# Conv and routed attention on one core: each pair of heads in its own half of the array

## The reference

```python
x = conv3x3(quantize(x), sign(W) * mean|W|) + b
xn = layernorm(x, g1, b1)
q, k, v = split(xn @ wqkv + bqkv)            # 64 channels each
qr, kr, vr = to_regions(q, k, v)             # 49 regions (7x7) of 64 pixels (8x8)
idx = top_k(mean(qr) @ mean(kr).T, 4)        # 4 key regions for each query region
scores = einsum(qh, kh[idx]) / sqrt(8)       # 8 heads of 8 channels, 64 queries x 256 keys
x = x + (softmax(scores) @ vh[idx]) @ wo + bo
x = x + gelu(layernorm(x, g2, b2) @ w1 + bm1) @ w2 + bm2
```

## Time and profile before

| what | value |
|---|---|
| median of three runs | 5610.56 us |
| profiled execution, its own time | 5625.85 us |
| its span | 5623.2 us |
| mean granted TensorE clock | 0.898 |
| 98 steps of a pair, from the first score product at 247.4 us on | about 338 us |

### The profile page before, as it was taken

The page is one execution under the profiler, slowest core; times in us unless marked ns, Lnnn a source line. Parts: engine busy times, 40 slices in busy tenths (PEclk is TensorE's granted clock), DMA queues, the critical chain, the costliest instruction groups (busy, mean ns, idle before and its releaser), DMA issues.

```text
span 5623.2 us, 182695 instructions
## 1 busy us (share of the span) xinstructions
PE 4720.9 (84%) x43666; PEld 3049.9 (54%) x43666; DVE 3648.9 (65%) x8855; ACT 3287.3 (58%) x6282; POOL 2777.4 (49%) x9656
## 2 busy tenths in 40 slices
PE   2388888888889898888888889888888888888888
PEld 1265555655556555555555556555565655556564
DVE  2266666766667666676766667666676766667676
ACT  1156556565665756556565665656556565665657
POOL 1245455454554645455454554545455464554553
PEclk9589899988889989898989999989899998999989
DMA  2333343333423334243333423334233333423311
GB/s 61 95 99 92 82 109 75 94 84 91 108 68 102 82 93 103 72 109 83 96 87 89 109 69 101 82 94 104 71 110 88 94 84 92 111 65 106 83 45 33
DMA packets 626961, 494.05 MB, mean 88 GB/s; under 512 B 483792, under 2 KB 613968, under 8 KB 615536
## 3 DMA queue, kind: packets, MB, share of 16 engines
q10 hardware_dynamic: 335360, 212.04, 16.6%
q1 hardware_dynamic: 290416, 268.94, 16.5%
HBM read 268.80 MB, written 211.94 MB: 85 GB/s over the span
## 4 chain that ended last, share of the span: by engine, by line
PE 52%; DMA 13%; issue 9%; ACT 7%; DVE 6%; DVEq 4%; SPq 4%; ACTq 3%; POOL 2%; POOLq 0%
PE ps L1003 11%; PE ps L1033 9%; PE ps L1017 8%; DMA max_d<-tr 6%; PE ps L896 5%; DMA qm<-qk_d 3%; DVEq L223 3%; PE ps L953 3%; ACTq L237 2%; PE ps L989 2%; PE ps L916 2%; PE ps L912 2%; DMA xin<-in_x 2%; ACT pt L847 2%; PE ps L974 2%
## 5 line engine op out<-in xcount | busy, mean ns | idle before, releaser
L736 DVE TENSOR_REDUCE mx<-ps 128x4 f32<-128x1024 f32 x1568 | 1921.6, 1225 | 1396.2 <-PE ps L1003 1128.7
L847 ACT ACTIVATE pt<-ps 128x512 f32<-128x512 f32 x3136 | 1694.2, 592 | 875.0 <-PE ps L1017 811.9
L505 POOL COPY vg<-vs 64x72 f32 x6272 | 1563.5, 249 | 781.6 <-POOL kg L490 576.7
L1003 PE MATMUL ps<-kg,qm 96*128 96x256 f32 x6272 | 1358.3, 342 | 364.4 <-DVE mx L736 112.2
L490 POOL CAST kg<-ks 96x128 fp32r x3136 | 845.2, 295 | 1550.5 <-PE ps L1017 1195.5
L1003 PEld LDWEIGHTS ps<-kg,qm 96*128 96x128 f32 x6272 | 963.3, 206 | 1087.2 <-issue 889.0
L1017 PE MATMUL ps<-qm,kg 97*128 97x256 f32 x6272 | 1126.5, 303 | 151.7 <-ACT pt L847 96.9
L1033 PE MATMUL ps<-pt,vg 128*32 128x128 f32 x25088 | 1092.0, 294 | 51.8 <-DVE um L726 39.1
L1017 PEld LDWEIGHTS ps<-qm,kg 97*128 97x128 f32 x6272 | 940.2, 206 | 214.6 <-ACT pt L847 154.7
L1033 PEld LDWEIGHTS ps<-pt,vg 128*32 128x32 f32 x25088 | 629.5, 114 | 296.5 <-issue 58.0
L645 DVE CAST kg<-ks 96x128 fp32r x3136 | 630.9, 244 | 137.9 <-issue 132.4
(11 more groups left out here) (113 smaller groups left out, 4036.1 us busy)
## 6 DMA issues: line engine op xcount, KB each, us to landing
qk_d<-stg SPq DMA_DIRECT2D x224, 448.0 KB, 3.6
qm<-qk_d ACTq DMA_DIRECT2D x1792, 42.0 KB
ks<-qk_d ACTq DMA_DIRECT2D x96, 784.0 KB, 6.3
vs<-v_d ACTq DMA_DIRECT2D x64, 882.0 KB, 7.1
xin<-in_x SPq DMA_DIRECT2D x119, 224.0 KB, 2.6
xi_d<-xi SPq DMA_DIRECT2D x112, 224.0 KB, 2.7
qk_d<-stg SPq DMA_DIRECT2D x112, 224.0 KB, 3.2
max_d<-tr SPq DMA_DIRECT2D x1568, 2.0 KB
```

The lines of the kernel that those rows point to most:

```text
L505: j = pool.tensor_copy(vg[slot][rows, (k // 2) * VW:(k // 2 + 1) * VW], vs[place(m)[0]][rows, bass.ds(region, 1), :].rearrange("p o n -> p ...
L736: v.tensor_reduce(mx[h % 2][:].rearrange("p (g j e) -> p g j e", g=2, j=2)[:, :, :, 0], ps[:, 0:2, :].rearrange("p g (j k) -> p g j k", j= ...
L847: act.activation(pt[m % 2][:, c], ps[:, 2 + c, :], ACT.Exp, scale=float(HD) ** -0.5).then_inc(S["pt_ready"], 1)
L1003: i = pe.matmul(ps[:, g, 256 * j:256 * j + 256], qm[c % 2][0:NP3, t, g, 2 * j:2 * j + 2, :].rearrange("p h t -> p (h t)"), kg[slot][0:NP3, ...
```

## The change

Heads are taken in pairs. A pair takes 48 rows (`NP3` = 3 * 2 * 8), and the two pairs of a group lie in the two halves of the array: rows 0 to 47 and 64 to 111 (`HALF` = 64). `qm` becomes half as large: in each half it has column blocks for two heads. `ks` has its rows in the same places, and its unused rows are set to -1, so the copies into `kg` now take all 128 rows and bring the -1 rows (48 and 112) with them. `scores` still issues four products, now of 48 rows, where consecutive ones lie in different halves and write different banks. `turned` issues eight products of 49 rows with 128 moving columns in place of four of 97 rows with 256; a bank now belongs to a half of the array, not to two of the key regions, so all eight must be done before either bank is full, and they start only when both banks' exps of the step before are done. The keys come in six DMAs in place of three, issued every step and not every second step. The row of largest scores goes to two rows of 256 numbers.

```diff
--- before.py
+++ after.py
@@ -28,7 +28,8 @@
 EPS = 1e-5
 HG = 4
 NG = HEADS // HG
-NP3 = 3 * HG * HD
+HALF = 64
+NP3 = 3 * 2 * HD
 VC = 18
 VW = 4 * VC
 
@@ -49,7 +50,7 @@
 ROUTE_AT = 62
 A_LOAD, B_LOAD = 70, 6
 QK_DMAS, V_DMAS = 3, 4
-KV_DMAS = 5
+KV_DMAS = 8
 
 
 def p_item(h):
@@ -141,7 +142,7 @@
 
         ks = [sb(f"ks{i}", [128, NG, R, RT], F32R) for i in range(2)]
         vs = [sb(f"vs{i}", [128, R, VW]) for i in range(2)]
-        qm = [sb(f"qm{i}", [128, NW, NG, HG, RT], F32R) for i in range(2)]
+        qm = [sb(f"qm{i}", [128, NW, NG, 2, RT], F32R) for i in range(2)]
         kg = [sb(f"kg{i}", [128, NG, TOPK, RT], F32R) for i in range(RING)]
         vg = [sb(f"vg{i}", [128, 2 * VW + 16]) for i in range(RING)]
         mx = [sb(f"mx{i}", [128, 32]) for i in range(2)]
@@ -234,16 +235,18 @@
             i, s = c // NW, c % NW
             src = qk_d[bass.ds(q, 1), i, 0:C, :, ST * s:ST * s + ST].rearrange("o (g h d) q (s t) -> g h (o d q) s t", g=NG, h=HG, s=NW)
             for g, h in heads:
-                eng.dma_start(qm[c % 2][24 * h:24 * h + 24, :, g, h, :].bitcast(F32), src[g, h]).then_inc(q_loaded[c % 2], 16)
+                row = HALF * (h // 2) + 24 * (h % 2)
+                eng.dma_start(qm[c % 2][row:row + 24, :, g, h % 2, :].bitcast(F32), src[g, h]).then_inc(q_loaded[c % 2], 16)
 
         def keys_values(eng, q, i, n):
 
-            if n < 3:
-                src = qk_d[bass.ds(q, 1), i, C:2 * C, n // 2, :].rearrange("o (g c) n -> (o c) g n", g=NG)
-                dst = ks[i][n:NP3:3].rearrange("p g r t -> p g (r t)").bitcast(F32)
+            if n < 6:
+                part, term = n // 3, n % 3
+                src = qk_d[bass.ds(q, 1), i, C:2 * C, term // 2, :].rearrange("o (g j c) n -> j (o c) g n", g=NG, j=2)[part]
+                dst = ks[i][HALF * part + term:HALF * part + NP3:3].rearrange("p g r t -> p g (r t)").bitcast(F32)
             else:
                 src = v_d[bass.ds(q, 1), i].rearrange("o t r n -> (o t) (r n)")
-                dst = vs[i][64 * (n - 3):64 * (n - 3) + 64].rearrange("p r n -> p (r n)")
+                dst = vs[i][64 * (n - 6):64 * (n - 6) + 64].rearrange("p r n -> p (r n)")
             eng.dma_start(dst, src).then_inc(kv_loaded[i], 16)
 
         def loads(eng, p, h, kind):
@@ -259,14 +262,14 @@
                 if h == A_LOAD:
                     staged_all(eng, p + 1)
                     gathered(eng, p, R)
-                if 0 <= h - A_LOAD < 2 * KV_DMAS and (h - A_LOAD) % 2 == 0:
-                    keys_values(eng, p + 1, 0, (h - A_LOAD) // 2)
+                if 0 <= h - A_LOAD < KV_DMAS:
+                    keys_values(eng, p + 1, 0, h - A_LOAD)
             local = h if kind == "lead" else h - STEPS
             if local >= 0 and kind != "last":
                 if local == B_LOAD and kind != "lead":
                     gathered(eng, p, STEPS)
-                if 0 <= local - B_LOAD < 2 * KV_DMAS and (local - B_LOAD) % 2 == 0:
-                    keys_values(eng, p if kind == "lead" else p + 1, 1, (local - B_LOAD) // 2)
+                if 0 <= local - B_LOAD < KV_DMAS:
+                    keys_values(eng, p if kind == "lead" else p + 1, 1, local - B_LOAD)
 
         def first_loads(eng):
 
@@ -361,8 +364,8 @@
 
                     sp.wait_ge(hopped[m % 2], (p * R + m // 2 + 1) * 16)
                     settled(sp)
-                    sp.dma_start(qm[m // NW % 2][NP3:NP3 + 1, m % NW].rearrange("o g h t -> o (g h t)").bitcast(F32),
-                                 max_d[m % RING].rearrange("j p -> (j p)").unsqueeze(0)).then_inc(row_ready[m % RING], 16)
+                    sp.dma_start(qm[m // NW % 2][NP3:128:HALF, m % NW].rearrange("o g e t -> o (g e t)").bitcast(F32),
+                                 max_d[m % RING].rearrange("(j g) p -> j (g p)", j=2)).then_inc(row_ready[m % RING], 16)
                 if live(h, kind):
 
                     sp.wait_ge(S["tr_ready"], T + 1)
@@ -487,8 +490,8 @@
                     pool.wait_ge(kv_loaded[i], (p + m // STEPS + 1) * (16 * KV_DMAS))
                     settled(pool)
                 for k, region in enumerate(chosen(m, 2)):
-                    j = pool.tensor_copy(kg[slot][0:NP3, :, 2 + k, :],
-                                         ks[place(m)[0]][0:NP3, :, bass.ds(region, 1), :].rearrange("p g o t -> p g (o t)"))
+                    j = pool.tensor_copy(kg[slot][:, :, 2 + k, :],
+                                         ks[place(m)[0]][:, :, bass.ds(region, 1), :].rearrange("p g o t -> p g (o t)"))
                 j.then_inc(S["kp_ready"], 1)
 
             def values(p, m, kind):
@@ -589,8 +592,8 @@
                 v.memset(t[:], 1.0)
             for t in qm:
                 v.memset(t[:].rearrange("p s g h t -> p (s g h t)").bitcast(F32), 0.0)
-            for t in kg:
-                v.memset(t[:].rearrange("p g k t -> p (g k t)").bitcast(F32), -1.0)
+            for t in ks:
+                v.memset(t[:].rearrange("p g r t -> p (g r t)").bitcast(F32), -1.0)
             link(v.memset(rx[:], 0.0))
             v.memset(epst, EPS)
             v.memset(mean_w[0:64, 0:64], 1.0 / C)
@@ -642,8 +645,8 @@
                     settled(v)
                 gather_ready(v, p, m)
                 for k, region in enumerate(regions(v, regs, m, 0, 2)):
-                    j = v.tensor_copy(kg[slot][0:NP3, :, k, :],
-                                      ks[place(m)[0]][0:NP3, :, bass.ds(region, 1), :].rearrange("p g o t -> p g (o t)"))
+                    j = v.tensor_copy(kg[slot][:, :, k, :],
+                                      ks[place(m)[0]][:, :, bass.ds(region, 1), :].rearrange("p g o t -> p g (o t)"))
                 j.then_inc(S["kd_ready"], 1)
 
             def strip_ahead(q, h):
@@ -1000,9 +1003,9 @@
                     pe.wait_ge(S["mx_ready"], T)
                 for g in range(NG):
                     for j in range(2):
-                        i = pe.matmul(ps[:, g, 256 * j:256 * j + 256],
-                                      qm[c % 2][0:NP3, t, g, 2 * j:2 * j + 2, :].rearrange("p h t -> p (h t)"),
-                                      kg[slot][0:NP3, g].rearrange("p k t -> p (k t)"), start=True, stop=True)
+                        d = slice(HALF * j, HALF * j + NP3)
+                        i = pe.matmul(ps[:, j, 256 * g:256 * g + 256], qm[c % 2][d, t, g].rearrange("p e t -> p (e t)"),
+                                      kg[slot][d, g].rearrange("p k t -> p (k t)"), start=True, stop=True)
                 i.then_inc(S["sm_full"], 1)
 
             def turned(p, m):
@@ -1010,14 +1013,17 @@
                 T = p * STEPS + m
                 c, t, slot = m // NW, m % NW, m % RING
                 pe.wait_ge(row_ready[slot], (p * 14 + c + 1) * 16)
+                if not (isinstance(T, int) and T == 0):
+                    pe.wait_ge(S["pt_ready"], (T - 1) * 2 + 2)
                 for b in range(2):
-                    if not (isinstance(T, int) and T == 0):
-                        pe.wait_ge(S["pt_ready"], (T - 1) * 2 + b + 1)
                     for g in range(NG):
-                        i = pe.matmul(ps[:, 2 + b, 256 * g:256 * g + 256],
-                                      kg[slot][0:NP3 + 1, g, 2 * b:2 * b + 2, :].rearrange("p k t -> p (k t)"),
-                                      qm[c % 2][0:NP3 + 1, t, g].rearrange("p h t -> p (h t)"), start=True, stop=True)
-                    i.then_inc(S["st_full"], 1)
+                        for j in range(2):
+                            d = slice(HALF * j, HALF * j + NP3 + 1)
+                            n = 256 * b + 128 * g
+                            i = pe.matmul(ps[:, 2 + j, n:n + 128], kg[slot][d, g, 2 * b:2 * b + 2, :].rearrange("p k t -> p (k t)"),
+                                          qm[c % 2][d, t, g].rearrange("p e t -> p (e t)"), start=True, stop=True)
+                            if b == 1 and g == 1:
+                                i.then_inc(S["st_full"], 1)
 
             def attended(p, m):
 
@@ -1032,7 +1038,7 @@
                     for j in range(4):
                         i = pe.matmul(ps[32 * j:32 * j + 32, 4, 128 * u:128 * u + 128],
                                       vg[slot][:, c * VW + VC * j:c * VW + VC * j + 32],
-                                      pt[m % 2][:, c, 128 * j:128 * j + 128], start=c == 0, stop=c == 1)
+                                      pt[m % 2][:, j % 2, 256 * c + 128 * (j // 2):256 * c + 128 * (j // 2) + 128], start=c == 0, stop=c == 1)
                 i.then_inc(S["u_full"], 1)
 
             def step(p, h, kind):
```

## The result

The changed kernel is slower: 6057.71 us (median of four runs, 6021.98 to 6092.67) against 5611.55 us in the same comparison, a ratio of 1.079 with a 95% interval of 1.0721 to 1.0859. The forecast was 5490 us, range 5340 to 5690. The profiled execution took 6092.67 us with a span of 6090.9, and its mean granted TensorE clock is 0.780, where it was 0.898.

What follows compares the result with a forecast made beforehand. Bound: TensorE's written order in full steps, a 2.2 us loop in short ones, SyncE's queue close behind. Terms -222 - 55 + 33 + 75 + 30 + 10 + 5 = -124 us from 5625.85, adjusted to the median: 5490 us, range 5340 to 5690.

Steps and rivals of the forecast that it cites:

- (a): Scores block: four products run two by two in the array's halves, 0.24 us less a block, -222 us.
- (b): Turned block: eight 128-column products in pairs, only the last product shorter, 0.07 us less, -55 us.
- (c): Changes of array shape around scores and turned: 0.21 us each for drain and unhidden load, net +33 us.
- the fourth case: TensorE in steps full of products: lower-clock share rises, 11 us each point, 5705 us at 40%; slower, chance 16%.
- (f): DMA issues: six key loads for three on ScalarE, +10 us; maxima row in two pieces 0, up to 0.23 us.
- (d): SyncE's queue of maxima stores and row loads: its 2.12 us floor a step takes back gain, +75 us.
- (e): Turned waits for the previous step's second exp and hands over both banks at the end: +30 us.
- (g): Constants set at the start: 16.5 us against 11.2, the weights wait for it, +5 us.

Runs made afterwards that it cites:

- the twins at the end: Kernel before with 127 and 128 rows plus both DMA costs of the change: 5760.17 us; changed kernel with filled rows and wide turned products: 5801.94 us.

## Why the prediction was wrong

(a) was right in its size: 0.23 us between the starts of scores and turned, 0.24 forecast. (b) too: 0.09 us, 0.07 forecast, with turned's loads starting in pairs 0.11 to 0.12 us apart. (c) as well: behind L980, full height, the new scores end 0.43 us later (2803.75 to 2804.18), which is the old 0.46 less 0.24 plus the 0.21 of the change of shape. Behind L992, of half height like the scores, the median is 0.24 us and was 0.67 before. The work of the blocks was read correctly, and it decided nothing.

The step that failed first is the clock: the sum of -124 us has no term for it, and it stood only in the fourth case, "the clock falls", at 16%. It came: 0.898 to 0.780, so 20% of the time at the lower level became 44%. The price put there, 11 us for each point, gives 264 us. Measured, the changed kernel stands 242 us above the one with only its DMA costs (6058 against 5816), after whatever the halves won, and 256 us came back by filling rows and columns alone. So the chance was far too low, and the price rather low too: the runs that change only rows or columns read 14 to 23 us for each point (112 us for 0.039 of clock in the kernel before, which is 7.8 points of time at the lower level; 142 for 0.031, 143 for 0.036, 256 for 0.083 in the changed one). The 242 us are then what is left after the blocks' gain. The argument against the case, that the page's slices stay at 8 or 9, spoke of a kernel whose scores and turned took 96 and 97 rows. That turned's products stream for half of a round, 128 columns behind a load of 128, stood in (b) as costing nothing. Streaming 256 in half of the rounds gave back 143 us and filling turned's rows 142, so both the columns not streamed and the rows left empty had a price.
The Trainium skill (TensorE: Matmul & The Clock Gate, section on what is actually happening) has the gate set by how busy the engine has been. The rows here agree only in part: the page of the profile shows 80% busy in the changed kernel both at 49 rows and at 64, with the clock at 0.780 and 0.811, and in the kernel before 84% at 96 and 97 rows and 82% at 127 and 128, with the clock at 0.898 and 0.937.

The second is (f). "The row of maxima in two pieces ... 0, and up to the 0.23 us of another issue": the issue grew by 0.27 us in each step, a little over the upper end. Its price in the same sentence, 360 us if it counted everywhere, was too high, and 0 too low: 150 us for a somewhat longer issue (0.59 us) in the kernel before. It was in the text and not in the sum. The key loads' landing stood there too, with no cost: "in smaller pieces, and the last now lands a little earlier". Half a load takes nearly as long as a whole one, and the six cost 52 us in the kernel before. There the last packet of the values does end earlier, about 37 us after the start of the load stage's first maximum (40 to 41 before), but the last of the keys later, 27 us (25). What in those stages waits for this isn't shown.

(d) rightly put the limit into SyncE's queue, but with the old floor of 2.12 us; with the longer issue it is 1.67 + 0.69 = 2.36 us. One or two short steps in a row do go faster, against (d), since the maximum waits only for the store of two steps ago: 144 of the gaps between two maxima are 2.00 to 2.05 us, and before none was under 2.1. Then the queue is behind and TensorE waits, as in the stretch above. SyncE's wait for VectorE fell only from 939 to 862 us, so by its own sign (d) isn't confirmed. (e): the waits for exp doubled (312 us in 258 waits, 155 in 253 before), at about the same number; what the hand-over costs alone wasn't tried and stays open. (g): the constants' ks part is

```profile
10.69 5.29 DVE L596 MEMSET ks<- 128x6272 f32 x1 [1.25 <-issue]
17.23 5.29 DVE L596 MEMSET ks<- 128x6272 f32 x1 [1.26 <-issue]
```

with gaps of 1.25 us and not 0.7, and the first maximum starts at 259.5 us, 248.7 before: 11 us, 5 forecast. With only the key loads split it starts at 252.5, so some 4 of the 11 are the loads'.

The account as it stands: 5620 us, 193 for the DMAs (both measured in the kernel before), and 242 for the halves with their clock, which is what is left to the measured 6058 and so no check of it. Filled rows and columns take off 256, a little more than the 242. Not settled is how the clock's share divides between rows left empty, columns not streamed and waiting gaps: each of three different means raised it, and they weren't crossed fully. The 42 us between the twins at the end are placed, in the load stages at a lower clock, but not explained; the late hand-over of both banks, the constants and the twin's own details are in it.

## What to carry to other kernels

A change that makes TensorE's products smaller must be priced at the granted clock it leaves behind, not only at the high one: look where the engine will wait after the gain, and what the next block costs at the lower level. Where rows stand empty and the clock row is below full, try filling them with zeros first; here that gave 2% for a change of slice bounds and of one row's place. Price each small DMA of a full queue by its issue time with its new pattern of partitions; 0.36 us more in each step came with 2.7%.

## What was not expected of the hardware

- The granted clock rose from 0.898 to 0.937 when score products took 127 and 128 rows in place of 96 and 97, and from 0.780 to 0.811 with 64 in place of 49 in one block, though the added rows of the query tile hold zeros.
- A DMA of one row to two rows of the query tile is issued in 0.24 us if they are neighbours and in 0.59 us if they are 16 apart (0.50 us for two rows of 256 numbers 64 apart).
- A key load of 16 partitions and 392 KB lands in 6.0 us (5.3 in the kernel before with split loads), one of 32 partitions and 784 KB in 6.3.
